# B's rows of a selective scan read back from DRAM on all partitions, streams started one behind the other, and spare buffers moved, in a 16-part network on one core

## The reference

```python
x = x + scan(_layernorm(x))        # L0_attn_a
x = x + experts(_layernorm(x))     # L0_ffn, then L0_attn_b (linear attention), L0_ffn again
...                                # L1: gated linear attention, local attention x2 around attention
x = x + scan(_layernorm(x))        # L2_attn_a, then L2_ffn, L2_attn_b, L2_ffn
...                                # L3: block attention, slots, grouped attention, slots
```

```python
h = 0.0
for t in range(L):
    # x_t, dt_t: [batch, 256]; B_t, C_t: [batch, 16]; A: [256, 16]
    A_bar = 1.0 + A * dt_t[..., None]        # exp(A * dt_t) in L2
    h = A_bar * h + B_t[:, None, :] * dt_t[..., None] * x_t[..., None]
    y_t = sum(C_t[:, None, :] * h, axis=-1)
```

## Time and profile before

| | |
|---|---|
| median of 3 executions | 4108.95 us (4104.8 to 4114.81) |
| the profiled execution | 4107.76 us, of which the span of the core's instructions is 4106.5 us |
| mean granted TensorE clock | 0.918 of full speed |
| busy: PE, DVE, ACT, GpSimd (POOL) | 3566.6, 2524.6, 2365.9, 1204.4 us |
| instructions | 47919 |
| DMA | 91.60 MB, queues busy 8% |

### The profile page before, as it was taken

The page is one execution under the profiler, slowest core; times in us unless marked ns, Lnnn a source line. Parts: engine busy times, 40 slices in busy tenths (PEclk is TensorE's granted clock), DMA queues, the critical chain, the costliest instruction groups (busy, mean ns, idle before and its releaser), DMA issues. The chain is left out here.

```text
span 4106.5 us, 47919 instructions
## 1 busy us (share of the span) xinstructions
PE 3566.6 (87%) x16336; PEld 1728.2 (42%) x16336; DVE 2524.6 (61%) x5892; ACT 2365.9 (58%) x5149; POOL 1204.4 (29%) x1004
## 2 busy tenths in 40 slices
PE   4769999899988899988888886689999999888886
PEld 1324434343334554534445442234434444454344
DVE  5896532424568767657776788975455435655574
ACT  4555662727455666656666666575364643665674
POOL 3463223231134644213553454631000000001230
PEclk8899999999989999979999998999998999977896
DMA  3000000000000001020000001000221002302310
GB/s 136 0 0 1 0 1 1 1 0 0 1 1 1 1 1 48 27 67 19 1 1 1 1 1 52 1 0 1 57 65 35 7 23 55 85 19 50 79 44 11
DMA packets 83181, 91.60 MB, mean 22 GB/s; under 512 B 26680, under 2 KB 72440, under 8 KB 80888
## 3 DMA queue, kind: packets, MB, share of 16 engines
q1 hardware_dynamic: 82936, 88.53, 7.7%
HBM read 61.66 MB, written 25.43 MB: 21 GB/s over the span
## 5 line engine op out<-in xcount | busy, mean ns | idle before, releaser
L334 ACT ACTIVATE scratch<-psum 128x512 f32<-128x512 f32 (+6 forms) x2004 | 958.3, 504 | 1053.9 <-PE psum L306 938.3
L345 POOL TENSOR_TENSOR scratch<-scratch 128x512 f32<-128x512 f32 (+3 forms) x536 | 689.2, 1293 | 1527.0 <-ACT scratch L334 1244.0
L306 PE MATMUL psum<-scratch,w_experts 128*128 128x512 f32 (+3 forms) x2192 | 1050.8, 609 | 37.3 <-ACT scratch L334 23.1
L306 PE MATMUL psum<-scratch 128*32 128x128 f32 (+13 forms) x6112 | 712.5, 346 | 92.4 <-ACT scratch L334 27.9
L345 DVE TENSOR_TENSOR scratch<-scratch,psum 128x512 f32<-128x512 f32 (+2 forms) x732 | 460.9, 635 | 378.0 <-PE psum L306 370.0
L334 ACT ACTIVATE scratch<-scratch 128x255 f32<-128x255 f32 (+11 forms) x1264 | 550.0, 463 | 135.5 <-DVE scratch L369 45.3
L306 PEld LDWEIGHTS psum<-scratch,w_experts 128*128 128x128 f32 (+3 forms) x2192 | 390.5, 189 | 517.1 <-issue 404.1
L306 PEld LDWEIGHTS psum<-scratch 128*32 128x32 f32 (+7 forms) x6112 | 371.9, 137 | 441.3 <-issue 251.5
L306 PE MATMUL psum<-scratch,w_constants 128*128 128x512 f32 (+2 forms) x848 | 454.8, 631 | 28.4 <-DVE scratch L345 16.5
L357 DVE TENSOR_TENSOR_SCAN scratch<-scratch 128x512 f32<-128x512 f32 x256 | 367.1, 1435 | 75.3 <-POOL scratch L345 75.3
L334 ACT ACTIVATE scratch<-psum,w_experts 128x512 f32<-128x512 f32 x256 | 173.0, 686 | 295.5 <-PE psum L306 294.9
(11 more groups left out here) (97 smaller groups left out, 3679.0 us busy)
## 6 DMA issues: line engine op xcount, KB each, us to landing
q_stack<-scratch SPq DMA_DIRECT2D x72, 192.0 KB, 2.7
scratch<-q_out SPq DMA_DIRECT2D x96, 96.0 KB
q_out<-scratch SPq DMA_DIRECT2D x40, 192.0 KB, 3.0
scratch<-q_stack SPq DMA_DIRECT2D x24, 288.0 KB
w_local<-q_stack SPq DMA_DIRECT2D x16, 288.0 KB
scratch<-q_out SPq DMA_DIRECT2D x24, 192.0 KB
w_experts<-q_out SPq DMA_DIRECT2D x24, 192.0 KB
w_experts<-L_experts_dram SPq DMA_DIRECT2D x1, 4356.0 KB, 13.2
```

The costliest lines, as they stand in the source:

```text
L306: return self.engine.matmul(out, lhsT, rhs, start=start, stop=stop, **kw)
L334: return self.engine.activation(out, src, function, **kw)
L345: return self.engine.tensor_tensor(out, a, b, op)
```

## The change

1. **Scans.** ACT copies rows 0 to 15 of the product with `w_bc` (B in fp32, 16 x 256) to `b_rows`; SP writes them to a DRAM tensor `b_out` and reads them back, up to three rows (128 x 768 columns) per DMA, with every partition given the same rows, into one of two `rings`. GpSimd takes B from there. PE spreads only C, one product instead of two per step; the ACT copy of a B row is gone. `h` has three buffers. The decay of step n waits for the scan of n-2 and no longer for its product with C.
2. **Streams** start one behind the other: stream j at `added` of the first sequence of stream j-1's first scan.
3. **Spare buffers.** The second local part of a stream borrows a slice of `w_early`, not of `w_experts` or the same one as the first; `w_early` is laid out with gaps for it (`FROM`), so that the load of `L2_experts` waits for part 6 instead of 7 and `L2_attn` borrows after part 7 for all streams. Constants that nothing uses are left out (2714 to 2072 columns), and `SCRATCH` is 6384.
4. **Costs in the planner.** `LATENCY` 80 instead of 90; an fp32 DMA counts 1/400 ns a byte. The semaphore name "stack" becomes "rows", shared by the DMAs of attention and scan.

```diff
-LATENCY, DMA_LATENCY, LOAD_LATENCY = 90, 2500, 20000
+LATENCY, DMA_LATENCY, LOAD_LATENCY = 80, 2500, 20000
-SCRATCH = 6400
+SCRATCH = 6384
...
-    ISSUE, FIXED, PER_BYTE = 410, 1500, 1 / 150
+    ISSUE, FIXED, PER_BYTE = 410, 1500, {F32: 1 / 400, BF16: 1 / 150}
...
 class Scan(Part):
-    D, N = 2, 16
+    D, N, READ = 2, 16, 3
...
-                    for i in range(2):
-                        row = i * N + n
-                        last = e.matmul(self.B2[:, i, :], over(self.m["row_of_32"][:, row:row + 1], [6 * N, P]), self.bc)
-                    last.then_inc(*self.post("spread", bt, n))
+                    e.matmul(self.b[:, 0:T], over(self.m["row_of_32"][:, N + n:N + n + 1], [6 * N, P]), self.bc).then_inc(*self.post("spread", bt, n))
...
             e.wait_ge(*(yield self["rank_bc", bt]))
+            e.activation(self.b_rows, self.b[0:N, 0:T], ACT.Copy).then_inc(*self.post("b_rows", bt))
             e.activation(self.low, self.a[0:self.rank, 0:T], ACT.Copy).then_inc(*self.post("low", bt))
...
                 if n >= 2:
-                    e.wait_ge(*(yield self["cmul", bt, n - 2]))
+                    e.wait_ge(*(yield self["scanned", bt, n - 2]))
...
-                e.wait_ge(*(yield self["spread", bt, n]))
-                e.activation(self.b_row[n % 2], self.B2[:, 0, :], ACT.Copy).then_inc(*self.post("b_row", bt, n))
...
                 e.tensor_tensor_scan(flat, a, flat, 0.0, ALU.mult, ALU.add).then_inc(*self.post("scanned", bt, n))
                 e.wait_ge(*(yield self["scanned", bt, n]))
-                e.tensor_tensor(h, h, over(self.B2[:, 1:2, :], [P, D, T]), ALU.mult).then_inc(*self.post("cmul", bt, n))
+                e.wait_ge(*(yield self["spread", bt, n]))
+                e.tensor_tensor(h, h, over(self.B2[:, 0:1, :], [P, D, T]), ALU.mult).then_inc(*self.post("cmul", bt, n))
...
             for n in range(N):
-                e.wait_ge(*(yield self["b_row", bt, n]))
-                if n >= 2:
-                    e.wait_ge(*(yield self["acc", bt, n - 2]))
+                r, i = divmod(n, self.READ)
+                e.wait_ge(*(yield self["rows", r % 2, bt, r]))
+                if n >= 3:
+                    e.wait_ge(*(yield self["acc", bt, n - 3]))
...
-                e.tensor_tensor(self.h[n % 2], self.dx, over(self.b_row[n % 2].unsqueeze(1), [P, D, T]), ALU.mult).then_inc(*self.post("bx", bt, n))
+                e.tensor_tensor(self.h[n % 3], self.dx, over(self.rings[r % 2][:, i:i + 1, :], [P, D, T]), ALU.mult).then_inc(*self.post("bx", bt, n))
+
+    def sp(self, e):
+        for bt in range(PER_STREAM):
+            rows = self.s.b_out[bt]
+            e.wait_ge(*(yield self["b_rows", bt]))
+            e.dma_start(rows, self.b_rows).then_inc(*self.post_dma("written", bt, "b"))
+            e.wait_ge(*(yield self["written", bt, "b"]))
+            for r in range(-(-self.N // self.READ)):
+                first = r * self.READ
+                count = min(self.READ, self.N - first)
+                if r >= 2:
+                    e.wait_ge(*(yield self["bx", bt, first - self.READ - 1]))
+                elif r:
+                    e.wait_ge(*(yield self["dt", bt]))
+                src = rows[first:first + count].unsqueeze(0).broadcast_to([P, count, TOKENS])
+                e.dma_start(self.rings[r % 2][:, 0:count], src).then_inc(*self.post_dma("rows", r % 2, bt, r))
...
-        self.second, self.freed_by = self.s.spare[self.group]
+        self.second, self.freed_by = next(self.s.spare[self.group])
...
-LATER = {"L2_experts": 7, "L2_attn": 7, "L3_blocks": 7, "L3_slots": 10, "L3_gqa": 10}
+LATER = {"L2_experts": 6, "L2_attn": 7, "L3_blocks": 7, "L3_slots": 10, "L3_gqa": 10}
+SPARE = HEADS8 // 2 * TOKENS // 2
+FROM = {"L1_attn": 3 * SPARE, "L2_scan": 4 * SPARE}
...
-            s.spare = {"L1_local": (mine, (2,)) if first else (pair[0], (3,)), "L1_attn": (*pair, (3,)),
-                       "L2_attn": (local[:, at:at + n], mine, (7,) if first else (7, 8)),
+            s.spare = {"L1_local": iter(((mine, (2,)) if first else (pair[0], (3,)), (mine, ((2,), (2,), (4,), (6,))[s.index]))), "L1_attn": (*pair, (3,)),
+                       "L2_attn": (local[:, at:at + n], mine, (7,)),
...
-            ready = (0, "load", "x") if first else parts[s.index - FIRST][0]["added", 0]
+            ready = (0, "load", "x") if s.index == 0 else parts[s.index - 1][0]["added", 0]
```

More of the change, by code:

```diff
@@ L632, in lay_out @@
         end, self.used = self.used, mark
[L633 to L636, removed]
+        self.b_rows = self.take(T, parts=N)
+        self.used = mark
+        rings = [self.take(self.READ, T)]
+        assert self.used >= end
+        self.decay, self.h = ([self.take(D, T) for _ in range(n)] for n in (2, 3))
+        mark = self.used
+        self.low, self.rest = self.take(T, parts=self.rank), self.take(T)
+        self.used = mark
+        self.rings = rings + [self.take(self.READ, T)]
         self.bc = self.take_bf16(T, parts=3 * 2 * N)
         self.A = self.take(D, N)
-        self.rest = self.take(T)
         self.A2, self.B2 = v2(self.a, T), v2(self.b, T)
@@ L1636, in sp_maxima @@
             slot = u % 2
-            e.wait_ge(*(yield self["stack", slot, u]))
+            e.wait_ge(*(yield self["rows", slot, u]))
             for i in range(3):
@@ L1698, in pe_start @@
         e.wait_ge(*(yield self["token", "v_tok"]))
[L1699 removed]
+        e.wait_ge(*(yield self["rows", 0, 0]))
     def heads(self, i):
@@ L1803, in sp @@
         m, shape = slice(self.max_row, self.max_row + 3), [3, self.HALF, TOKENS]
-        e.dma_start(self.k_rows[0][m], over(self.m["row_ones"].unsqueeze(1), shape)).then_inc(*self.post_dma("stack", 0, "ones"))
+        e.dma_start(self.k_rows[0][m], over(self.m["row_ones"].unsqueeze(1), shape)).then_inc(*self.post_dma("rows", 0, "ones"))
         yield from self.sp_parts(e)
@@ L1807, in sp @@
             e.wait_ge(*(yield self["written", bt]))
-        e.dma_start(self.k_rows[1][m], over(self.m["row_ones"].unsqueeze(1), shape)).then_inc(*self.post_dma("stack", 1, "ones"))
+        e.dma_start(self.k_rows[1][m], over(self.m["row_ones"].unsqueeze(1), shape)).then_inc(*self.post_dma("rows", 1, "ones"))
         yield [self.sp_stack(e), self.sp_maxima(e)]
@@ L2750, in build @@
         width = {g: packed_dram[g].shape[1] for g in groups}
-        shared = {}
+        shared, where_to = {}, {}
         for name, sets in (("early", (EARLY, LATE)), ("experts", (("L0_experts",), ("L2_experts",))),
                            ("local", (("L1_local",), ("L2_attn", "L3_blocks"))), ("constants", (("constants",),))):
-            n = max(sum(width[g] for g in some) for some in sets)
+            n = 0
+            for some in sets:
+                at = 0
+                for g in some:
+                    where_to[g] = max(at, FROM.get(g, 0))
+                    at = where_to[g] + width[g]
+                n = max(n, at)
             shared[name] = ctx.enter_context(nc.sbuf_tensor(f"w_{name}", [P, n], F32)), sets
```

45 lines of the change are left out of this document (20 added, 25 removed).

## The result

The changed kernel took **4060.15 us** (median of 4 runs, 4058.85 to 4061.83) against 4110.9 of the kernel before beside it (4104.8 to 4114.81): a ratio of 0.9878 [0.9861, 0.9895]. It is 50 us faster. 4042 was forecast; 4060 lies in the range, on the forecast's side of no change. The sum came out nearly right with two of its four terms (the head and the gate) outside the bounds given for them, so most of what follows is about the terms.

The account below looks back on a forecast made before the run. TensorE (PE), busy 87% of the span, was taken to set the pace. From 4107.8 us, -45 (head), -45 (second scans), +25 (tail) and 0 (gates) gave 4042.8, less a small load 4042; range 3970 to 4100.

Parts of the forecast that it names:

- A = -45: Head, first scans with chained streams: less lost PE time and fewer spreads save 45 us (bounds -15 to -75).
- with the looser chain I take 9%: Beside the remaining first scans, PE loses 9% of some 300 us, 27 us.
- the 128 of the first scans ... I take 24: Removing the first scans' 128 PE spreads of B is worth 24 us, from 15 to 38.
- B = -45: Second scans: DVE goes from 83% to 90% busy, 535 us in place of 580, saving 45 (0 to -86).
- D = 0: Spare buffers, weight gates and table: the earlier load of the second experts gains nothing now (-30 to +15).
- C = +25: Tail: 237 DVE rows behind stream 0's last add instead of 59; a fifth of 134 us charged (0 to +60).
- The rows come late: Rival: reads of B's rows exceed 6.6 us and DVE waits; 4177 us at 8 us a read; chance 0.12.
- GpSimd and DVE exclude each other: Rival: in the scans, products and scans take turns, 2.48 us a step; 4114 us, no change; chance 0.04.
- The tail and the gates take it back: Rival: the tail costs 60 us, head and second scans gain only 30 each; 4108 us, no change; chance 0.08.
- It mixes better: Rival: DVE fills up in both scan stages and the middle mixes better; 3983 us; chance 0.13.
- The change doesn't do what it says: Rival: spread of C or PE's sum stands as late as B's did, halving head and second-scan gains; 4087 us; chance 0.06.

Follow-up runs that it names:

- the gate at 7: Changed kernel with the load of the second experts waiting for part 7 of all streams again instead of 6, planned anew: 4099.78 us.
- the kernels at 569 and 587 us apart: 569: changed kernel, each stream starting when the previous one left its whole first scan, 4219.05 us; 587: kernel before with only the chained stream start, 4263.65 us.
- the doubling: Changed kernel in its own order, with a second, useless table load before each of the 215 explicit ones: 4207.18 us.
- the fastest kernel here: Changed kernel with the planner's LATENCY at 100 instead of 80, only the order differing: 4042.85 us.
- the runs with one piece each: Changed kernel with streams started in pairs as before: 4144.72 us; kernel before with only the streams started one behind the other: 4263.65 us.

## Why the prediction was near, term by term

- **"A = -45", the head.** Measured: 9 to 15 us in the first quarter. The chain of the single stream and its instants were right to some 3 us (96.4 and 181.7). The step that failed is "with the looser chain I take 9%" for PE's loss beside the remaining scans: it was 17% from 182 to 545, 60.5 us where 27 were forecast for a stretch of 300. The chain from GpSimd to DVE did get looser; the one between PE and DVE, product with C to next spread, didn't, and PE stood in it for 18.4 us. In this stretch ACT also loads tables 41 times, against 11 in the 177 us of before that the 12% came from; what that did here no run separates. DVE, whose pace gave the steps, was busy 77%. The second failure is "the 128 of the first scans ... I take 24": all 256 cost 12 or less when they were put back, so a spread next to another in the same wait is worth little here.
- **"B = -45", the second scans.** DVE went from 83% to 540.73/623 = 87%, 90 was forecast. Cut as the quarters above, the third quarter takes 999 us with the gate at 7 where it took 1027: -28 without the gate. The direction was right, the size about six tenths.
- **"D = 0", the gate.** The step said "no gain now, but with streams further apart a gate less", and then costed the first half of the sentence. With streams 386 us apart the second half held: 40 us by the medians, 41 in the third quarter (999 to 958). The reason given ("The last local part ends at 2473.5 and second scans run on till 2818.0") looked at the last stream; the one that waits is the first.
- **"C = +25", the tail.** 1062 to 1097, +35, within its bounds. Its premise held: the streams' last adds come at 3837, 3920, 4020 and 4058 us, 220 us from first to last, where they were 62 apart. A fifth of the DVE work behind stream 0's end was a guess all the same. In the kernels at 569 and 587 us apart the last eighth is 36 us above after's and 52 above before's.
- **ACT.** "The ACT copies lie beside ACT's idle time, so I cost them at nothing" was right for the copies, and the only thing said of ACT. The order of the changed kernel held 152 more table loads. At 0.68 us each, as measured in the doubling, they would be up to 100 us, spread over the terms above; that is an estimate and not shown, since 468 of them stand in the fastest kernel here and no run took them out of an unchanged order.
- **The sum.** -9 for A, -3 in the second quarter, -28 for B, -41 for the gate and +35 for C make -46, as the profiled spans differ. The forecast's -65 was near because a gain that hardly came (A) and one that wasn't counted (the gate) offset each other. That is luck, and not a good working that erred a little. It is luck too that the order drawn was this one: with LATENCY at 90 the same design takes 4107, outside the range.

The rivals. *The rows come late*: fell; no wait for a read in either scan stage, and reads of 3.0 us. *GpSimd and DVE exclude each other*: fell as to its price, since the single stream has a step of 2.39 us in the mean, and of 2.15 to 2.3 in nine of fifteen, where exclusion needed 2.48. *The tail and the gates take it back*: its tail came at +35, not +60, and the gate went the other way. *It mixes better*: DVE stayed at 77% and 87%. *The change doesn't do what it says*, since the spread of C stands late: its time (4087) didn't come, but its mechanism is what the stretch from 182 to 545 us shows in part. No rival held what the runs with one piece each show: that neither main edit gained by itself.

Still open: what the middle owes to the distance of the streams; why the order with 90 doesn't have the fast sixth eighth although its load goes out early; how much of the 4060 is the luck of one order; and what a planner that counts a table load's 0.68 us would give (not tried).

## What to carry to other kernels

Cut two executions at equal shares of the bounding engine's work, counted over the instructions that both have, not at the ends of stages: stage ends move with the change and put gains where there are none. For a gate that waits for all streams, ask when the *first* stream wants what it guards, and reckon it with the distance that the change itself brings about. Where a planner sets the order, compare several orders or issue the edit behind its back: here one constant moved the time by as much as the change, and neither main edit alone gained.

## What the runs showed of the hardware

- A table load on ACT is busy 1.283 us, and each of 215 added ones cost this kernel 0.68 us (147 in all), with ACT busy 62% before they were added.
- A read of 384 KB from three rows in DRAM to 128 partitions, 80 times beside 16 of 128 KB, ended at most 3.2 us after its issue where no other DMA was near, and was never waited for with three steps (6.6 us) of lead; the 16 KB write ahead of each set lands in 1.4 us (median).
- GpSimd's product and DVE's scan slow each other, but not by their whole lengths: a scan of 1.22 us and a product of 1.26 that never overlapped would need 2.48, and the 16 steps of the single stream came 2.39 apart in the mean; in the kernel before, 46 scans and 45 products ran in 100 us where 113 would be needed. The Trainium skill (SBUF — State Buffer, "Who interferes with whom") has the second one blocked. The traces agree that they hinder each other, and disagree that it lasts for the whole of the other's time; they don't exclude that a part of each is exclusive.
